# Four fused graph layers: a stage's tail reordered, two score tiles moved ahead, one subtraction moved between engines

## What is computed

```
x = x + L0(h)          # mean of the neighbours @ W_l.T + b_l + h @ W_r.T, relu; 20000 edges
h = norm, relu of x
x = x + L1(h)          # four blocks of conditioned norm, attention over the edges, conditioned norm, MLP
x = x + L2, x + L3     # a weighted graph convolution; an edge MLP with a scatter-add
```

```
y = norm(x) * (1 + cond @ sw + sb) + cond @ bw + bb
y = softmax over the edges of (q k) times v, @ wo + bo ;  x = x + y        # 4 heads of 128
y = norm(x) * (1 + cond @ sw2 + ...) + ... ; x = x + relu(y @ m_w1 + m_b1) @ m_w2 + m_b2
```

## Time and profile before

| | us |
|---|---|
| median of 3 runs | 1599.44 (1599.12 to 1599.72) |
| the profiled execution, own time | 1600.61 |
| its span, first to last instruction | 1597.4 |
| input layer | 0 to 172.5 |
| transformer, four blocks | 173.6 to about 800 |
| graph convolution, edge layer | to 1597.4 |

### The profile page before, as it was taken

The page is one execution under the profiler, slowest core; times in us unless marked ns, Lnnn a source line. Parts: engine busy times, 40 slices in busy tenths (PEclk is TensorE's granted clock), DMA queues, the critical chain, the costliest instruction groups (busy, mean ns, idle before and its releaser), DMA issues. The chain is left out here.

```text
span 1597.4 us, 26151 instructions
## 1 busy us (share of the span) xinstructions
PE 1511.4 (95%) x9086; PEld 1216.4 (76%) x9086; DVE 1187.2 (74%) x2049; ACT 1076.7 (67%) x1557; POOL 649.0 (41%) x471
## 2 busy tenths in 40 slices
PE   4998899999999999999999999999999999999987
PEld 4765587778787878787864578888888888888874
DVE  8995647564656465646634399999999999999967
ACT  8844536543654465445532289999999999999953
POOL 3430200110012001200300677888888888888501
PEclk9999899999999999999999999999999999999989
DMA  3002320013002300120104777777777777777610
GB/s 110 1 2 87 93 86 27 7 51 116 27 7 61 105 27 7 54 93 27 69 27 140 178 158 151 154 157 151 157 151 158 153 157 153 157 154 155 159 34 33
DMA packets 88590, 151.47 MB, mean 95 GB/s; under 512 B 23611, under 2 KB 28603, under 8 KB 88003
## 3 DMA queue, kind: packets, MB, share of 16 engines
q0 software_dynamic: 54400, 85.33, 27.2%
q1 hardware_dynamic: 34114, 65.15, 12.7%
HBM read 141.02 MB, written 9.31 MB: 94 GB/s over the span
## 5 line engine op out<-in xcount | busy, mean ns | idle before, releaser
L1876 POOL DMA_INDIRECT edge_gathered<-dst_table,edge_index x158 | 272.1, 1722 | 59.1 <-issue 37.2
L227 PE MATMUL edge_z2p<-edge_w_hi,edge_h_hi 128*128 128x512 f32 x628 | 252.3, 402 | 0.6 <-DVE edge_late L2243 0.6
L227 PE MATMUL edge_z2p<-edge_w_hi,edge_h_lo 128*128 128x512 f32 x628 | 247.9, 395 | 0.0
L227 PE MATMUL edge_z2p<-edge_w_lo,edge_h_hi 128*128 128x512 f32 x628 | 247.6, 394 | 0.0
L1848 POOL DMA_INDIRECT edge_gathered<-src_table,edge_index x158 | 175.1, 1108 | 83.8 <-issue 79.8
L1079 POOL TENSOR_TENSOR h<-h,tr_row_b 128x512 f32<-128x512 f32 x40 | 59.2, 1513 | 271.5 <-ACT C L1325 271.1
L1068 POOL TENSOR_TENSOR tr_cw<-w_c,tr_cw 32x1024 fp32r<-32x1024 f32 x7 | 16.6, 2372 | 318.8 <-ACT tr_cw L1285 318.8
L227 PEld LDWEIGHTS edge_z2p<-edge_w_hi,edge_h_hi 128*128 128x128 f32 x628 | 118.3, 188 | 32.5 <-issue 7.7
L227 PEld LDWEIGHTS edge_z2p<-edge_w_hi,edge_h_lo 128*128 128x128 f32 x628 | 118.2, 188 | 27.9
L227 PEld LDWEIGHTS edge_z2p<-edge_w_lo,edge_h_hi 128*128 128x128 f32 x628 | 118.3, 188 | 24.2
L1095 PE MATMUL tr_one<-tr_yT_hi,tr_w_hi 128*128 128x256 f32 (+2 forms) x384 | 119.3, 311 | 4.2 <-issue 4.2
(11 more groups left out here) (380 smaller groups left out, 3964.5 us busy)
## 6 DMA issues: line engine op xcount, KB each, us to landing
w_c<-in_attr_T SPq DMA_DIRECT2D x78, 128.0 KB
w_a<-in_wv SPq DMA_DIRECT2D x4, 1024.0 KB, 5.4
w_b<-in_wq SPq DMA_DIRECT2D x4, 1024.0 KB, 5.2
w_a<-in_wk SPq DMA_DIRECT2D x4, 1024.0 KB, 7.5
w_b<-in_wo SPq DMA_DIRECT2D x4, 1024.0 KB, 6.9
w_a<-in_m SPq DMA_DIRECT2D x4, 1024.0 KB, 5.2
w_b<-in_m SPq DMA_DIRECT2D x4, 1024.0 KB, 5.3
w_c<-in_cond_w SPq DMA_DIRECT2D x4, 768.0 KB, 5.5
```

What stands on the lines that cost most here:

```text
L227: mm = pe.matmul(out, a, b, start=(n == 0), stop=(n == last))
L1876: pool.indirect_dma_start(out=from_rows[ring][:, j, :].bitcast(F32), out_offset=None, in_=k.dst_table, in_offset=bass.IndirectOffsetOnAxis ...
```

## The change

It has three parts.

1. **The input layer's tail is merged.** The degree products move ahead of the last three aggregates, between the fifth aggregate and the rest; the condition products come after the aggregates, right before `left`. VectorE makes all five sums of W and four of the five no-edge pairs before it takes `hidden`, the fifth pair after it; it takes `degT` after the sigmoid, and `cond` after that. ScalarE sums counts and takes the first four aggregates before the exponential of the sigmoid. The split of the conditioning weights for block 0, s = 0, moves from the start of the transformer to here: ScalarE's copy after its last exponential, VectorE's subtraction in front of `left`. The target is a tensor of its own, `cw_first`, that both stages see; its memory later serves the edge layer's h1_lo. noise, ph, turns and cond_rows share memory.
2. **Scores among the key products.** The scores of tiles 0 and 1 (`AMONG` = 2) are made after the key products (f = 1, m = 1) and (1, 2). VectorE masks them, and scales tile 0, in the same places. The loop starts making scores at n = 2.
3. **The low part for the next block's first norm** is made by VectorE, in two pieces of 32 x 512 in the steps n = 12 and 13 of the attention, in place of GpSimd's 32 x 1024. GpSimd keeps s = 1.

```diff
@@ TensorE, input layer
+                aggregate(*AGG[AHEAD])
+                bank = plan.open(pe, ("degT", 0))
...
+                for m, f in AGG[AHEAD + 1:]:
+                    aggregate(m, f)
+                pe.wait_ge(silu_ready, 1)
+                for f in range(2):
+                    bank = plan.open(pe, ("cond", f))
@@ ScalarE, input layer
+                for i in range(AHEAD):
+                    if i >= 2:
+                        act.wait_ge(has_ready, i - 1)
                     sum_counts(i)
-                    take_agg(*AGG[i - 1])
+                    take_agg(*AGG[i])
+                act.wait_ge(cz_ready, 2)
+                act.activation(ce[:, :], cz[:, :], ACT.Exp, scale=-1.0).then_inc(ce_ready, 1)
...
+                act.wait_ge(k.cw_loaded, 16)
+                act.activation(k.cw_first, k.w_c[0:CROWS, 0:2, :], ACT.Copy).then_inc(logs_ready, 1)
@@ VectorE, input layer
+                for i in range(NT):
+                    sum_W(i)
+                for i in range(NT - 1):
+                    no_edge(i)
                 for f in range(2):
                     bank = plan.take(dve, ("hidden", f))
...
+                dve.wait_ge(logs_ready, NT + 2)
+                rest = slice(PART, 2 * PART)
+                own(dve.tensor_tensor(k.cw_first[rest, :, :], k.w_c[rest, 0:2, :], k.cw_first[rest, :, :].bitcast(F32),
+                                      ALU.subtract))
@@ transformer: GpSimd, ScalarE, VectorE
-                        if b < LAST:
+                        if b < LAST and s == 1:
                             pool.wait_ge(bias_added, of_norm(b, s, NT - 1))
                             cut(b + 1, s)
...
-                cut(0, 0)
+                act.sem_inc(cw_high, 1)
...
+                def cond_low(b, piece):
+
+                    rows, part = slice(PART, 2 * PART), cw[0][PART:2 * PART, piece, :]
+                    dve.wait_ge(cw_high, b * 2 + 1)
+                    ins = dve.tensor_tensor(part, cw_raw[rows, piece, :], part.bitcast(F32), ALU.subtract)
+                    own(ins) if piece == 0 else ins.then_inc(cw_ready, 1)
...
-                dve.wait_ge(cw_high, 1)
-                rest = slice(PART, 2 * PART)
-                dve.tensor_tensor(cw[rest, 0:2, :], cw_raw[rest, 0:2, :], cw[rest, 0:2, :].bitcast(F32),
-                                  ALU.subtract).then_inc(cw_ready, 1)
+                dve.sem_inc(cw_ready, 1)
@@ transformer: the attention, TensorE and VectorE
                                 by_feature(name, m, f, wts, b)
+                                if name == "k" and f == 1 and 0 <= m - 1 < AMONG:
+                                    score(b, m - 1)
...
+                            if f == 1 and 0 <= m - 1 < AMONG:
+                                masked(b, m - 1)
+                                if m >= 2:
+                                    shared_out(b, m - 2)
...
+                        if AMONG <= n < N:
+                            masked(b, n)
+                        if n >= AMONG:
+                            shared_out(b, n - 1)
...
+                        if n in (12, 13) and b < LAST:
+                            cond_low(b + 1, n - 12)
```

More of the change, by code:

```diff
@@ L784, in no_edge @@
                     own(dve.tensor_tensor(k.logc[:, i, :], k.logc[:, i, :], k.C[:, i, :], ALU.add))
-                for i in range(3):
+                for i in range(NT):
                     sum_W(i)
+                for i in range(NT - 1):
+                    no_edge(i)
+                for f in range(2):
+                    bank = plan.take(dve, ("hidden", f))
+                    ins = dve.tensor_scalar(cz[:, f * HALF:(f + 1) * HALF], bank[0:COND, 0:HALF], fb1[:, 0:1], None, ALU.add)
+                    plan.took(("hidden", f), ins)
+                plan.need(dve, ("hidden", 1))
+                dve.sem_inc(cz_ready, 2)
+                no_edge(NT - 1)
                 dve.wait_ge(ce_ready, 1)
@@ L791, in _ @@
                 dve.tensor_tensor(cz[:, :], cz[:, :], ce[:, :], ALU.mult).then_inc(silu_ready, 1)
-                for i in range(3, NT):
-                    sum_W(i)
+                bank = plan.take(dve, ("degT", 0))
+                plan.took(("degT", 0), dve.tensor_scalar(k.rdeg[:, :], bank[:, 0:NT], 1.0, None, ALU.max))
+                plan.need(dve, ("degT", 0))
+                step(dve.reciprocal(k.rdeg[:, :], k.rdeg[:, :]))
                 dve.wait_ge(has_ready, NT)
@@ L1148, in value, with score @@
                     by_node("v", i, of_tile(rows, i), "wv", b)
+                def score(b, n):
+                    h, i = divmod(n, NT)
+                    bank = plan.open(pe, ("S", b, n))
+                    if (b, n) == (0, 0):
+                        pe.wait_ge(pads_ready, 1)
+                    if i == 0:
+                        plan.need(pe, ("q", b, h, 1))
+                        plan.need(pe, ("k", b, h, 1))
+                    for f in range(2):
+                        mm = pe.matmul(bank[:, f, 0:PART_A], qT[:, h, i * P:(i + 1) * P],
+                                       kT[:, h, f * PART_A:(f + 1) * PART_A], start=True, stop=True)
+                    plan.made(mm)
                 for b in range(BLOCKS):
@@ L1167, in _ @@
                     for n in range(N + 4):
[L1168 to L1179 removed]
+                        if AMONG <= n < N:
+                            score(b, n)
                         if 2 <= n < N + 2:
@@ L1498, in attended, with masked, shared_out @@
                                                                 oT_hi[:, h, half].bitcast(F32), ALU.subtract))
+                def masked(b, n):
+                    i = n % NT
+                    bank = plan.take(dve, ("S", b, n))
+                    settle(k, dve)
+                    ins = dve.tensor_tensor_reduce(out=cols(scores[n % 2][:, 0:USED], PART_A), in0=bank[:, :, 0:PART_A],
+                                                   in1=cols(k.logc[:, i, 0:USED], PART_A), scale=-1.0, scalar=3.0e38,
+                                                   op0=ALU.add, op1=ALU.min, accum_out=nmax[:, n:n + 1])
+                    plan.took(("S", b, n), ins)
+                def shared_out(b, m):
+                    dve.wait_ge(exp_ready, b * N + (m + 1))
+                    own(dve.reciprocal(den[:, m:m + 1], den[:, m:m + 1]))
+                    own.wait()
+                    dve.tensor_scalar(probs[m % 3][:, 0:USED], probs[m % 3][:, 0:USED], den[:, m:m + 1],
+                                      k.has[:, m % NT:m % NT + 1], ALU.mult, ALU.mult).then_inc(probs_ready, 1)
                 own(dve.memset(qT[:, :, USED:NP], 0.0))
```

91 lines of the change are left out of this document (26 added, 65 removed).

## The result

The changed kernel took 1580.26 and 1582.17 us, against a median of 1599.28 (1598.73 to 1599.72) for the kernel before, run beside it: a ratio of 0.9889, with a 95% interval of 0.9873 to 0.9905, so 17.8 us less (15 to 20). The forecast was 1582.8, its range 1577.5 to 1588.5. Two further executions beside them took 5054.7 and 3362.9 us; none of the later executions was like them, why these two were isn't known, and they are left out.

The account below looks back on a forecast made before the run. TensorE, busy 95% of the span, was taken as the bound. Gains of 7.9, 1.25, 1.2, 2.4 and 3.9 us sum to 16.65, taking 1599.44 to 1582.8 us; range 1577.5 to 1588.5.

Parts of the forecast that it names:

- The tail: Input layer's end: reordered work lets VectorE reach the second left product at 150.3 instead of 158.27; gain 7.9 us, bounds 6.5 to 8.4.
- the 0.8 us of slack: Left products: VectorE may be 0.8 us late at the first tile for nothing; its work takes 2.6 us of 3.43.
- rival (a): Input layer's tail: VectorE's conditioning chain ends later than the first left product beyond the slack, giving back 1 to 3 us; chance 0.12.
- The transformer's start: Before the first scale products: ScalarE's copy and VectorE's subtraction no longer stand in front; gain 1.25 us, bounds 0.9 to 1.3.
- The clock: After the hole before the transformer: less TensorE time at half speed; gain 1.2 us, the middle, bounds -0.5 and 3.0.
- The early scores: Attention: two scores made among the key products start masking and exponentials sooner; 0.6 us a block, 2.4 in all.
- The low part: Attention, blocks 0 to 2: GpSimd's subtraction no longer stretches VectorE's scaling; 1.3 us a block, 3.9 in all.
- (b): Attention: early scores give nothing, ScalarE's saturated steps absorbing them; 1585.2 us, chance 0.10.
- (d): First attention steps: TensorE's clock falls to the lower level, costing 6.8 us a block; 1610 us, chance 0.03.
- (e): Left products and scaling: holes move whole to the next wait, stretched scaling not due to GpSimd; about 1597 us, chance 0.03.
- Rival (c): Transformer's start and attention: more gained through a short low clock and 1.2 us a block; 1578.6 us, chance 0.10.
- forecast's zero for the input layer's head: Up to the first aggregate: unedited stage carried over unchanged, gain 0.

Follow-up runs that it names:

- the filled hole: Changed kernel plus unread products in TensorE's hole between the left products and the transformer's first scale product; 1579.87 us, 0.9886 of the kernel before.
- the early low part: Changed kernel with VectorE's low pieces in steps 6 and 7 instead of 12 and 13, ScalarE's copy in step 2; 1584.97 us, 0.9916 of the kernel before.
- the tail alone: Changed kernel with early scores off and the low part back on GpSimd; 1587.57 us, 0.9933 of the kernel before.
- the join kernels: Changed kernel with the last block's five x + r additions moved from GpSimd to VectorE: 1577.56 us; the same plus unread products in the transformer-start hole: 1577.16.

## Why the prediction held, and where it did not

**The tail** was right in mechanism and size: 7.7 for 7.9. The left products began at 143.00 for 143.3, the second was taken at 150.17 for 150.3, but all of this profile stood 0.4 us earlier from the first aggregate on, which is not the change's doing. One step in it was wrong. It said that VectorE reaches `hidden` at 129.2, cover just enough; VectorE took it at 130.54. The W sums, beside which the text had put GpSimd's two bias additions, kept their pace (3.75 us for five); the additions ran on beside the no-edge pairs, whose steps took 1.78 and 1.55 us where the free ones took 0.82 and 0.48. The text had called the collision a microsecond or two and put it ahead of the condition vector, with 4 us of cover. That cover took it: silu ended at 138.4, where about 137.3 was forecast, and TensorE asked at 141.76. VectorE's own chain ended 0.27 us ahead of the first left product (0.1 in the forecast), so the 0.8 us of slack was not drawn on, and rival (a) was about 1.1 us away.

**The transformer's start** gave 1.37 for 1.25, and the experiment that puts the split back returned exactly before's 18.13.

**The clock** came out as 1.0 for 1.2, and that the number fits is in part luck. The forecast had no reason for a length between 6.8 and 13.65 us and took the middle of the two gains; in the changed kernel's three profiles the stretch lasted 10.2 us, in six of its variants 13.7. It ended 8.3 us after the first scale product, where 10.75 was before; that part cost some half a microsecond for each, as the forecast's step took it. But the step priced all of the low time so, and the filled hole shows 0.6 us for the first 6.2. The upper bound of 3.0 was built in part from time that would have been cheap.

**The early scores** gave 0.7 us a block for 0.6, 2.8 to 3.0 for 2.4. The path was as forecast. ScalarE's order of time in block 1, changed kernel, the exponentials of tiles 3 and 4:

```profile
381.19 0.82 ACT L1399 ACTIVATE hT<-hT,tr_nmax 128x626 f32<-128x626 f32 x1
...
383.50 0.82 ACT L1399 ACTIVATE hT<-hT,tr_nmax 128x626 f32<-128x626 f32 x1 [0.29 <-DVE tr_nmax L1531]
```

The third score starts at 377.32 here and at 390.01 before, 12.69 later. Shifted by that, tile 3's stands at 393.88, where 394.0 was worked out and the earlier trace rows has 394.89. Tile 4's stands at 396.19. The next row of before's exponentials has 396.81, so 0.6 of the 1.0 survives ScalarE's busy steps, as forecast:

```profile
396.81 0.81 ACT L1380 ACTIVATE hT<-hT,tr_nmax 128x626 f32<-128x626 f32 x1
```

The run with one early score shows that the gain needs the second.

**The low part** gave 4.0 for 3.9 over the whole stretch, 3.7 of it in the loops, and its cover was real: the same pieces where VectorE isn't idle cost 1.06 a block. A piece took 0.68 us; the forecast's 0.65 is not the half of 1.22 that it is called, which is 0.61. The stage table's 7.2 for both parts is 0.2 to 0.4 above what the two later profiles of the changed kernel give (522.29 and 522.46 for 522.07).

**What the sum left out** are two stages carried over unchanged. The hole of 2.19 us in the last block, which before has as well, now brought a low stretch (782.9 to 786.3) and 1.6 us with it; the forecast put the clock's risk into the attention and looked for none here. In return, the low stretch of before at 907.4 was absent from this profile, and TensorE's wait for the first gathered rows fell from 3.4 to 2.4 us; half of 3.4 and 1.0 make about the 2.6 to the end. In the second and third profile of the changed kernel a stretch of 3.4 us appears near 892 again, but there the low stretch of the last stage lasts 10.2 us instead of 13.7, and the end takes 737.97 and 737.86. Windows of before, of the changed kernel and of its second profile:

```profile
1542.30:1556.00 13.70, 10.84 (x43) 9.28 (x44) 7.12 (x14) 3.14 (x4) 0.00 (x0) 0.50 0.00 0
```

```profile
1523.50:1537.20 13.70, 11.09 (x44) 9.26 (x45) 6.68 (x13) 2.70 (x4) 0.00 (x0) 0.50 0.00 0
```

```profile
892.20:895.60 3.40, 3.40 (x9) 2.23 (x8) 1.55 (x3) 2.32 (x3) 2.79 (x3) 0.50 0.93 151
1527.10:1537.30 10.20, 7.59 (x32) 6.26 (x31) 5.72 (x11) 1.50 (x3) 0.00 (x0) 0.50 0.00 0
```

So each of the three is spared one low stretch of 3.4 us that the one profile of before has. Nothing in the change explains it, and before's profiled execution was itself 1.2 us above its median. The loss of 1.6 and the gain of 2.6 nearly cancel, by luck. Rivals (b), (d) and (e) fell: the scores gave 0.7 a block, the clock stayed up through all four attentions, and no hole moved on. Rival (c) named a gain of 20.85 us, and the profiled gain is 18.8, but not by its two causes.

**What stays open.** The parts don't add up in medians: early scores gave 4.3 and 4.0 us by the two pairs of medians, 2.8 to 3.0 by the stages. Of the rest, 1.0 lies ahead of every edit: in both profiles without early scores the aggregates begin at 118.31, in the three of the changed kernel at 117.20 to 117.36, though the code up to there is the same. It is lost over several of TensorE's steps in the count products. Why one program and not the other loses it wasn't found; the other variants, with that same code, lie anywhere from 117.22 to 118.32. The forecast's zero for the input layer's head is thus good to 1 us only.

## What to carry to other kernels

Where an engine has two jobs and one of them has no idle time behind it, the order of the jobs is worth the whole stall (here 7.7 us of 17.8); check each moved instruction against the idle time at its new place, not against the engine's average load. An addition given to GpSimd is not free for being off the path: look at what VectorE does in those microseconds, at the old place and the new. Early work helps only once enough of it is early that the next instruction of the queue no longer waits.

## What the runs showed of the hardware

**GpSimd beside VectorE costs both.** GpSimd's two bias additions took 2.50 us before, with VectorE idle beside them, and 5.02 in the changed kernel with VectorE at work:

```profile
121.87 5.02 POOL L384 TENSOR_TENSOR front_own_part<-front_own_part,front_bl 128x512 f32<-128x512 f32 x2 [13.60 <-ACT front_own_part L450]
```

The Trainium skill (GPSIMD Engine Reference, "1. Specifications") says that contention is with VectorE instructions of two SBUF inputs or in a mode that uses both ports; the rows agree for the two-input additions into logc, 1.78 for 0.82, and one-input steps were stretched too (1.55 for 0.48, and 2.54 for 0.61 in the scaling), in a mode that no row shows. The two-input W sums, 3.75 us for five, were not stretched; the first of the two GpSimd additions, which began beside them, took 3.21 us instead of 1.28.

**The clock falls after short holes, and not always.** A hole of 2.2 us was followed by a low stretch of 3.4 us in the last block of the changed kernel's three profiles, in those of the kernels with the split put back and the early low part, and in one of the two without early scores. In five others (the tail alone, the low part on GpSimd, the filled hole, one early score, and the other one without early scores) the same hole passed at full clock, as it did before. In the join kernels, which don't have the hole, there was none. After the hole at the transformer's start, where nothing filled it, the stretch lasted 10.2 or 13.7 us in the changed kernel and its variants, and began between 163.3 and 165.2.

The Trainium skill (TensorE: Matmul & The Clock Gate, "What's actually happening") says that the monitor is free-running; that one program, no early scores, had a low stretch at 788.7 in one profile and none there in the other agrees with it.
